# Second cross attention with six heads shifted by ScalarE, and the block tables and late routes moved around the first chunk of experts

## The reference, cut to what matters

```python
# layer 1: cross attention, 16 heads of width 8, 77 keys, layer norms on q, k and v
sim = einsum('bhqd,bhkd->bhqk', qh / sqrt(dk), kh)
weights = softmax(sim + NEG_BIAS * (~mask), axis=-1)
out = einsum('bhqk,bhkd->bhqd', weights, vh)

# layer 2, feed-forward: causal self attention over a latent, then top-2 of 8 experts
x = x + _mla(_rmsnorm(x, g1), Wq, Wdkv, Wuk, Wuv, Wo)
logits = _rmsnorm(x, g2) @ gate_w          # top_k = 2, softmax over the two
hid = silu(einsum('td,edh->teh', t, w1)); ye = einsum('teh,ehd->ted', hid, w2)
x = x + einsum('te,ted->td', combine, ye)

# layer 3, cross attention: k = rope(ctx @ w_k + b_k), v = ctx @ w_v + b_v, 77 keys
```

## Time and profile before

| what | value |
|---|---|
| median of 3 runs | 1088.34 us (1085.9 to 1089.47) |
| the profiled execution | 1098.73 us, of which its span 1096.9 us |
| PE busy | 941.7 us (86%) |
| DVE busy | 805.2 us (73%) |
| ACT busy | 531.4 us (48%) |
| POOL busy | 496.4 us (45%) |

### The profile page before, as it was taken

How to read it: one execution, slowest core, us unless ns; L and a number is a source line. 1 busy time by engine, 2 the same in 40 slices (tenths; PEclk the granted TensorE clock), 3 DMA queues, 4 the chain that set the end, 5 groups by cost and what they waited for, 6 DMA issues and landing times.

```text
span 1096.9 us, 19658 instructions
## 1 busy us (share of the span) xinstructions
PE 941.7 (86%) x6481; PEld 671.2 (61%) x6481; DVE 805.2 (73%) x2077; ACT 531.4 (48%) x1301; POOL 496.4 (45%) x451
## 2 busy tenths in 40 slices
PE   6999985777778999869987598989977999989987
PEld 4787543666577989737775243434435777668773
DVE  5889999999756777769995375776726544599962
ACT  3675555454434455734441166766753333455523
POOL 6445454556056564525655776574523300024420
PEclk9999895999879999969998669989999999999989
DMA  9200000000111111500000322222002000000001
GB/s 341 114 1 1 2 5 1 1 1 1 40 35 43 37 40 33 156 11 1 0 1 0 104 72 78 57 80 55 22 1 97 1 1 1 1 1 1 1 1 38
DMA packets 29827, 40.54 MB, mean 37 GB/s; under 512 B 11468, under 2 KB 25036, under 8 KB 29228
## 3 DMA queue, kind: packets, MB, share of 16 engines
q1 hardware_dynamic: 27244, 34.28, 9.9%
q0 software_dynamic: 2496, 5.16, 1.8%
HBM read 31.44 MB, written 7.82 MB: 36 GB/s over the span
## 4 chain that ended last, share of the span: by engine, by line
PE 51%; issue 19%; DVE 16%; POOL 9%; ACT 3%; DMA 2%; SPq 1%; DVEq 0%; POOLq 0%; ACTq 0%
PE ps L785 7%; PE ps L888 7%; POOL att L1757 4%; PE ps L1151 4%; PE ps L821 4%; PE ps L1123 4%; PE ps L811 4%; PE ps L1135 3%; PE ps L900 3%; PE ps L758 3%; PE ps L737 2%; DVE mx L2074 2%; DVE stats L1968 2%; DVE rs L2088 2%; DVE x L2437 2%
## 5 line engine op out<-in xcount | busy, mean ns | idle before, releaser
L1757 POOL TENSOR_TENSOR att<-att,ri 128x1232 f32<-128x1232 f32 x64 | 176.9, 2764 | 210.0 <-DVE ri L2094 210.0
L785 PE MATMUL ps<-VW,PT 128*128 128x128 f32 (+3 forms) x1280 | 160.2, 281 | 25.3 <-DVE x L2109 23.4
L785 PEld LDWEIGHTS ps<-VW,PT 128*128 128x128 f32 (+1 forms) x1280 | 150.9, 194 | 43.7 <-DVE x L2109 36.0
L1340 ACT ACTIVATE PT<-ps 128x512 f32<-128x512 f32 x128 | 70.3, 594 | 105.1 <-PE ps L758 104.4
L1332 ACT ACTIVATE att<-att 128x1232 f32<-128x1232 f32 x64 | 78.9, 1233 | 53.3 <-DVE att L2081 53.2
L758 PE MATMUL ps<-W,att 128*128 128x128 f32 (+1 forms) x640 | 85.1, 278 | 15.3 <-POOL att L1757 13.8
L1731 POOL TENSOR_TENSOR rstd<-ve,minus_half 128x4 f32<-128x4 f32 x38 | 38.8, 1034 | 125.4 <-DVE ve L1983 100.7
L2088 DVE TENSOR_REDUCE rs<-att 128x16 f32<-128x1232 f32 x64 | 91.2, 1426 | 0.4 <-ACT att L1332 0.4
L888 PE MATMUL ps<-PT,att 128*128 128x128 f32 x624 | 81.4, 286 | 9.4 <-issue 8.6
L821 PEld LDWEIGHTS ps<-U,att 128*128 128x128 f32 x512 | 66.7, 192 | 32.0 <-issue 26.8
L2534 DVE CUSTOM_DVE_ANT_0 C<-ps,cmaskb 128x512 bf16<-128x512 f32 (+1 forms) x128 | 71.0, 555 | 20.3 <-PE ps L1123 17.5
(11 more groups left out here) (425 smaller groups left out, 2090.1 us busy)
## 6 DMA issues: line engine op xcount, KB each, us to landing
U<-in_ffn SPq DMA_DIRECT2D x1, 6176.0 KB, 23.1
U<-split SPq DMA_DIRECT2D x144, 32.0 KB
W<-split SPq DMA_DIRECT2D x144, 32.0 KB
W<-in_packed SPq DMA_DIRECT2D x1, 2162.5 KB, 23.7
U<-in_ffn SPq DMA_DIRECT2D x1, 2060.0 KB, 8.1
U<-in_moe SPq DMA_DIRECT2D x1, 2048.0 KB, 7.4
split<-VBD SPq DMA_DIRECT2D x4, 384.0 KB, 2.9
split<-W SPq DMA_DIRECT2D x4, 384.0 KB, 2.7
```

Of the source, the lines that this page charges most:

```text
L785: q = mm(attended(s, t), PT[0:m, t.slot(2), c, :], batch(VW, t.group)[0:m, c * D:(c + 1) * D], start=(c == 0), stop=(c == NC - 1))
L1340: go(PT[:, t.slot(2), 4 * k:4 * k + 4, :].rearrange("p c n -> p (c n)"), ps[:, k0 + k, :], ACT.Copy).then_inc(probsT, 1)
L1757: tt(p, p, over_keys(ri[:, t.slot(2), :]), ALU.mult).then_inc(probs, 1)
```

## The change

**In X1** the last 6 of 16 heads are no longer shifted or summed by DVE. `largest` writes the negated maximum; `shift` adds it on 10 heads (770 columns); ACT takes the exponential of each of the other 6 heads by itself (77 columns each) with the negated maximum as bias and the sum as accumulator output, then one exponential over 770 columns; `total` sums 10 heads. `total` now stands behind `largest` in DVE's order.

**At the seam of MLA and MOE** batch 2's `rows` go from k = 67 to k = 64 (its normed rows on DVE from k = 64 to 61) and its `route` from k = 70 into chunk 0 (after unit 2). The last `route` goes from unit 7 to 6, `choose_experts(1)` from expert 3 to 2. `keys_values(X3)` is split into its products and copies at k = 71 to 73 and, after unit 1 of chunk 0, the third product. On POOL the wait for `w_ready` 4 now stands ahead of the block value tables.

```diff
-                                              ("rows", 16, 35, 0, B), ("route", 16, 38, 0, B)):
+                                              ("rows", 16, 35, 0, 2), ("rows", 16, 32, 2, 3), ("rows", 16, 35, 3, B),
+                                              ("route", 16, 38, 0, 2), ("route", 16, 44, 2, 3), ("route", 16, 38, 3, B)):
...
+        SPLIT = H - 6
...
                         down(c, u - 1)
+                        if c == 0 and u == 1:
+                            keys_values(X3, 2)
+                        if c == 0 and u == 2:
+                            beside("route", B - 2)
                         if c == 0 and u == 4:
                             beside("rows", B - 1)
-                        if c == 0 and u == 7:
+                        if c == 0 and u == 6:
                             beside("route", B - 1)
...
-                if k == 16 * B + 6:
-                    keys_values(X3)
+                if k in (16 * B + 7, 16 * B + 8):
+                    keys_values(X3, k - 16 * B - 7)
...
                 def exponent(t):
+                    if s == X1:
+                        act.wait_ge(rowmax, t.n + n0 + 1)
+                        act.wait_ge(probsT_ps, t.n * 3 + 3 * n0 + 3)
+                        wait(act, recip, t.n + n0 - 1)
+                        for h in range(SPLIT, H):
+                            keys = slice(h * KEYS, (h + 1) * KEYS)
+                            go(att[:, 2 + t.slot(2), keys], att[:, t.slot(2), keys], ACT.Exp,
+                               bias=mx[:, t.slot(2), h:h + 1], accum_out=rs[:, t.slot(2), h:h + 1])
+                        act.wait_ge(shifted, t.n + n0 + 2)
+                        go(att[:, 2 + t.slot(2), 0:SPLIT * KEYS], att[:, t.slot(2), 0:SPLIT * KEYS], ACT.Exp)\
+                            .then_inc(expd, 1)
+                        return
...
             starts(pool, MOE)
+            pool.wait_ge(w_ready, 4)
             pool.wait_ge(kv_sb, KV_SB0[X3] + 2)
             for b in range(B):
                 tt(heads(VBD3_at[b]), v3_s[:, b * KEYS:(b + 1) * KEYS].unsqueeze(1).to_broadcast([P, H, KEYS]),
                    over_keys(w("hm")), ALU.mult).then_inc(vbd, 1)
             pool.wait_ge(ld["e"], 32)
-            pool.wait_ge(w_ready, 4)
...
-                    v.tensor_reduce(top, src, AX.X, ALU.max).then_inc(rowmax, 1)
+                    v.tensor_reduce(top, src, AX.X, ALU.max, negate=s == X1).then_inc(rowmax, 1)
...
-                    if s in (X1, X2):
+                    if s == X1:
+                        tt(a[:, 0:SPLIT, :], a[:, 0:SPLIT, :], over_part(mx[:, t.slot(2), 0:SPLIT]), ALU.add).then_inc(shifted, 1)
+                    elif s == X2:
...
-                    v.tensor_reduce(rs[:, t.slot(2), :], heads(att[:, 2 + t.slot(2), :]), AX.X, ALU.add)\
+                    n = SPLIT if s == X1 else H
+                    v.tensor_reduce(rs[:, t.slot(2), 0:n], heads(att[:, 2 + t.slot(2), :])[:, 0:n, :], AX.X, ALU.add)\
...
-                if s in (X1, X2):
+                if s == X1:
+                    steps = [(add_to_scores, 0), (largest, 0), (total, 1), (invert, 1), (shift, 0)]
+                elif s == X2:
                     steps = [(add_to_scores, 0), (total, 1), (largest, 0), (invert, 1), (shift, 0)]
...
+                        if c == 0 and e == 0:
+                            beside("route", B - 2)
                         if c == 0 and e == 2:
                             beside("route", B - 1)
-                        if c == 0 and e == 3:
                             choose_experts(1)
...
-                if rest == 0 and 0 <= n < B - 1:
+                if rest == 0 and 0 <= n < B - 2:
                     rows_for_experts(n)
...
                 if k == 61:
                     weigh_experts(0)
+                    rows_for_experts(B - 2)
```

More of the change, by code:

```diff
@@ L455, in over_group_keys, with over_part @@
             return a.rearrange("p (g h) -> p g h", g=RG).unsqueeze(3).to_broadcast([P, RG, H // RG, KEYS])
+        SPLIT = H - 6
         def over_keys(a):
             return a.unsqueeze(2).to_broadcast([P, H, KEYS])
+        def over_part(a):
+            return a.unsqueeze(2).to_broadcast([P, SPLIT, KEYS])
         def fold_of(u):
@@ L670, in fold_values, with keys_values @@
                 t.then_inc(vw_ps, 1)
-            def keys_values(s):
+            def keys_values(s, part=None):
                 if s in (X0, X3):
@@ L676, in keys_values @@
                     k0 = 0 if s == X0 else 2
-                    mm(ps[:, k0, 0:CK], w(f"{l}wk"), w("ctxT"), start=True, stop=True).then_inc(kv_ps, 1)
-                    mm(ps[:, k0 + 1, 0:CK], w(f"{l}wv"), w("ctxT"), start=True, stop=True).then_inc(kv_ps, 1)
-                    pe.wait_ge(kv_sb, KV_SB0[s] + 2)
-                    if s == X3:
+                    if part in (0, None):
+                        mm(ps[:, k0, 0:CK], w(f"{l}wk"), w("ctxT"), start=True, stop=True).then_inc(kv_ps, 1)
+                    if part in (1, None):
+                        mm(ps[:, k0 + 1, 0:CK], w(f"{l}wv"), w("ctxT"), start=True, stop=True).then_inc(kv_ps, 1)
+                    if part in (2, None):
+                        pe.wait_ge(kv_sb, KV_SB0[s] + 2)
+                    if part == 2:
                         mm(ps[:, 2, 0:CK], w("rot"), k3_s, start=True, stop=True).then_inc(kv_ps, 1)
@@ L1294, in keys_values @@
                     act.wait_ge(*((ld["a"], 16) if s == X0 else (ld["e"], 32)))
-                    act.wait_ge(kv_ps, KV_PS0[s] + 1)
-                    go(k_to, ps[:, k0, 0:CK], ACT.Identity, bias=b_[:, 1:2]).then_inc(kv_sb, 1)
-                    act.wait_ge(kv_ps, KV_PS0[s] + 2)
-                    go(v_to, ps[:, k0 + 1, 0:CK], ACT.Identity, bias=b_[:, 2:3]).then_inc(kv_sb, 1)
+                    if part in (0, None):
+                        act.wait_ge(kv_ps, KV_PS0[s] + 1)
+                        go(k_to, ps[:, k0, 0:CK], ACT.Identity, bias=b_[:, 1:2]).then_inc(kv_sb, 1)
+                    if part in (1, None):
+                        act.wait_ge(kv_ps, KV_PS0[s] + 2)
+                        go(v_to, ps[:, k0 + 1, 0:CK], ACT.Identity, bias=b_[:, 2:3]).then_inc(kv_sb, 1)
                     if s == X0:
@@ L1666, in _ @@
                     gate_exp_moe(0)
-                if k == 16 * B + 6:
-                    keys_values(X3)
+                if k in (16 * B + 7, 16 * B + 9):
+                    keys_values(X3, (k - 16 * B - 7) // 2)
             hidden()
```

## The result

The changed kernel takes 1068.5 us (median of 4 runs, 1066.4 to 1071.05), the kernel before 1088.66 in the 4 runs beside them. The ratio is 0.9821, with a 95% interval of 0.9803 to 0.984: 20.2 us less, where 18.5 were forecast.

The account below looks back on a forecast made before the run. DVE was taken to bound X1, and PE's waits for norms, ACT and the chain ending MLA to count at the seam. X1's 10.8 us plus the seam's 7.75 made 18.5, from 1088.3 to 1069.8 us; range 1067 to 1079.

Parts of the forecast that it names:

- The bound of X1: X1's steady turns: DVE, busy without a gap, sets the 5.77 us turn until PE, ACT or POOL needs longer.
- DVE's turn: X1: shift and total save 0.48 us each, total's move costs nothing; 4.81 us, 4.9 with PE and POOL near misses.
- The head: X1 on ACT: one head's exponential with its sum costs 0.39 us, between 0.215 and 0.56.
- Rival (a): X1: ACT becomes the bound with a head near 0.5 us; turns of 5.3, time 1074.5 us; chance 0.20.
- X1's sum: X1: twelve shorter turns give 10.4 us, the last tile 0.4, the first four nothing; 10.8 us gained.
- End of MLA: Seam, before the experts: transposes for the last `out` start 3.55 us earlier, with the route and three products moved away.
- Chunk 0: Seam, first expert chunk: norms' wait, low clock and an ACT wait go, route and third product come in; 5.9 us gained.
- The tables, moved: Chunk 1: POOL's value tables stretch `rope_keys` to some 7 us; PE loses 1.7 us at the third `down`.
- (b): Seam: POOL's tables hit `rope_keys` and what follows for their whole 9 us; 7 us lost, time 1075; chance 0.09.
- (c): X1: POOL's product comes late and PE waits in every turn; turns of 5.4 us, time 1076; chance 0.07.
- (d): X1 on ACT: sums stop each activation until drained, a head over 0.74 us makes the kernel slower; chance 0.03.
- (e): No change: a head near 0.67 us, X1 loses 6.4, the seam gives 7.75; time 1087; chance 0.05.

Follow-up runs that it names:

- update run: Changed kernel with DVE's update step put between `total` and the reciprocal in X1; ratio 0.9821 to the kernel before.
- eight heads: Changed kernel with eight of X1's heads on ACT instead of six; ratio 0.9838 to the kernel before.
- the changed kernel's second trace: The changed kernel run again without any edit, on a third chip; 1078.30 us, ratio 0.9839 to the kernel before.
- seven heads: Changed kernel with seven of X1's heads on ACT instead of six; ratio 0.9816 to the kernel before.
- X1 alone: Only the diff's X1 part, with the old seam of MLA and MOE; 1078.34 us, ratio 0.9908 to the kernel before.
- tables-first run: Changed kernel with POOL's wait for the weights put back behind the four value tables; ratio 0.9855 to the kernel before.

## Why the prediction was right, and where its terms were off

The mechanisms held in both places. The sum of 18.5 us came near 20.2 with the help of errors that offset each other: X1 gave less than its term, the moved tables cost more than theirs, and the clock at the end of MLA, which is high in some traces and low in others with either seam, gave 1.25 us in this one.

**The bound of X1: right.** DVE's chain sets the turn before and after; no other engine took it over with six heads.

**DVE's turn: the mis-sized term.** The forecast was 4.81 us by sum and 4.9 with near misses; it is 5.04. The two shortened operations save 0.49 (`total` 1.43 to 0.94) and 0.50 (shift 1.40 to 0.90), a little more than the 0.48 each that were taken. What failed is the sentence that the new place of `total` costs nothing. It moves the maximum next to the addition whose result it reads, and the reciprocal next to `total`. The starts there are 1.46 us apart where the earlier trace rows has 1.35 from the addition to its then neighbour, and 0.97 where an independent neighbour has 0.86: 0.22 together. 5.77 - 0.99 + 0.22 = 5.00. The other 0.04 are two steps of 0.02 that the forecast doesn't name. The update run shows the second 0.11 by itself; the first was only read from the starts. The near misses of POOL and PE that the 0.1 was meant for did not occur: PE still waits 0.71 us for DVE in each turn, and DVE waits for neither.

**The head: right.** 0.344 us against 0.39 taken, bounds 0.215 and 0.56. The accumulator's record of 0.20 begins 0.25 after the head's own start, and the next head 0.095 after that; so the sum costs less than its record shows. Against the 0.215 us that the forecast took from the earlier trace rows with the sum free, it adds 0.13. The Trainium skill, page "ScalarE: Activation LUTs", section "What ACT_TABLE_LOAD costs", gives 280 ns + 0.833 ns a column for an activation with a bias column, which is 344 ns at 77 columns, and an overlap of about 93 ns. The trace's record is 358 ns in the mean of 96. By the page a head without its sum would be 0.25 us, and the sum would add about 0.09; both are estimates from its figures.

**Rival (a): its loop is there, its price is not.** ACT's turn is 4.3 us (51.56 us for twelve; the forecast's 2.3 + 6 x 0.344 makes 4.36), under DVE's. It takes the bound with eight heads or with `total` ahead of the maximum.

**X1's sum: too high.** Twelve turns give 12 x 0.735 = 8.8 us and not 10.4. The first three, counted at nothing, give 0.76 (3.82, 5.28, 6.25 against 4.31, 5.55, 6.25). That is 9.57, where 10.8 were forecast. Behind the last addition the trace has another 0.9, which would make 10.5; but that stretch takes 43.9 to 48.6 us in these kernels whatever their code, so the 0.4 us forecast for the last tile can't be read from it.

**End of MLA: right, with luck in the clock on top.** Forecast 3.55 us. PE's first `up` comes 794.97 - 790.29 = 4.68 us after the last weighting instead of 7.69, which is 3.0; the weighting itself ends 1.96 sooner after the second `write`. Some 0.7 of that is the `rows` put ahead, where 0.4 were forecast. The other 1.25 is the clock. Of the traces with the new seam some have it high in these first 8 us and some not. From the second `write`'s addition to the reciprocal of the last but one `out` it is 8.40 us in the changed kernel's second trace and 9.67 with seven heads:

```profile
787.91:796.00 8.09, 6.40 (x51) 2.11 (x49) 5.29 (x22) 6.29 (x18) 3.53 (x5) 1.00 0.00 0
```

```profile
786.54:795.30 8.76, 7.28 (x48) 1.85 (x45) 4.86 (x22) 6.01 (x18) 3.33 (x5) 0.81 0.01 2
```

The whole stretch to the first `up` is 16.90 us in the one kind and 18.15 in the other, against 21.87 before, where the clock was low too: the work saved is 3.7. X1 alone has the old seam and a high clock, 20.60 us, and 20.60 - 16.90 is 3.7 again.

**Chunk 0: right.** Forecast 5.9, measured 5.89. The four norms cover 0.88 us (1.2 had been named), PE doesn't wait for them, and the wait behind ACT's table loads is 0.63 instead of 1.67. The tables-first run shows that the wait and the clock behind it are the bulk of it, and that the clock's share (1.25 forecast) can be more than twice that. Against the chunk 0 of X1 alone, where the clock behind the old wait was low for longer, the gain is 6.8.

**The tables, moved: right in kind, too low in size.** `rope_keys` covers 8.0 us (forecast 7) and PE waits 2.44 once (forecast 1.7), at the `down` that was named. The last table ends 6.3 us after the chunk's start instead of 5.7, and the last key operation 0.34 behind it. Chunk 1 is 2.7 us longer in this trace and 4.35 where the clock fell behind the wait, which no term of the forecast has. The Trainium skill, page "SBUF — State Buffer", section "Who interferes with whom", says that DVE's two-port forms and GpSimd lock each other out for whole instructions, and that a DVE instruction with two SBUF inputs contends with a GpSimd one that reads SBUF, while one with at most one SBUF input doesn't. The trace agrees with both: the four norms at the old place, and every operation of `rope_keys` with its inputs in SBUF, end just behind a table, and the one with an input in PSUM keeps its 0.48 us. The price in these rows goes by the length of POOL's instruction: 1.90 to 2.43 us an operation beside tables of 2.3, 0.86 to 1.36 beside tables of 1.26. The mixing has two inputs in SBUF as well; it takes 1.23 us instead of 0.74, and no one waits for it.

Rivals (b), (c), (d) and (e) fell with this: the seam gave 8.9 us (7.0 by itself in time) and the tables took 2.7 to 4.35 of it, not 7; POOL's product covers 2.84 (forecast 3.0) and is not late; and the head costs half of what (d) needs.

## What to carry to other kernels

When an operation is moved in a full engine's order, ask who its new neighbours are: next to the producer of its input it costs 0.11 us each time here, and an unrelated step put between gives that back for nothing. Still the move can pay, because its place also sets how much time the other engine of the loop gets (0.37 us a turn here).

Work is split between engines until the second one fills: DVE fell by 0.16 us a turn for each head, ACT rose by 0.28 (0.344 less 77 columns of the large exponential), and the last head that shortened the turn was the seventh. Of POOL's long operations the shortest belong beside DVE's two-input work, and those without a reader soon come last; that order in POOL's queue, without any work removed, was worth 2.4 to 4.0 us in the traces.

A wait of PE can cost its length and the clock behind it: 4.3 us of wait came with 2.75 us of slow clock, and 2.44 us of wait came with 1.7 in four traces and with none in three. So two single traces of kernels that differ little can differ by the clock alone, and stages are compared at the same granted clock. And a profiled execution is compared with another stage by stage, since a stage that no one touched differed by 9.4 us.

## What the runs showed of the hardware that was not expected

- An activation with a sum as output leaves two records, 0.358 us for 77 columns and 0.20 for `ACTIVATION_READ_ACCUMULATOR`, but such heads start every 0.344 us.
- In X1's turn on DVE an instruction that reads its neighbour's result, behind a wait for the neighbour's semaphore, starts 0.03 us after the neighbour's covered time (210.05 to 210.08); one that doesn't starts 0.08 before its end.
- A 308-column DVE operation with its inputs in SBUF that meets one of POOL's tables ends 0.06 to 0.35 us behind it, whatever the table's kind: 2.43 us beside a value table, 1.36 beside a mask table, 0.48 with POOL idle.
- The same PE wait of 2.44 us in chunk 1 was followed by a granted clock of 1.00 in three traces and by a fall to the lower level in four (0.74 over the next 6.5 us with seven heads), which made the chunk 30.86 or 32.53 us long.
- The routed stage takes 126 us in the runs on one chip and 136 to 138 in those on two others, in every kernel alike, and 126.24 and 135.54 in two traces of one kernel. The granted clock over it is 0.95 in both. Whether the chip or the occasion sets it was not tried.
